# DVE normalises the three residual row tiles of a vision block, the context of tokens 3 and 4 is turned ahead of the later projections, and two orders change behind the router

## The chip, the core and the metric

The kernel runs on one core of a Trainium2 chip. The metric is the device time of one execution in microseconds. The core has TensorE (PE, matrix products and transposes, into eight PSUM banks), VectorE (DVE), ScalarE (ACT), GpSimd (POOL) and SyncE (SP, here the queue that issues most DMAs). Each engine runs its own instructions strictly in program order and waits on semaphores for the others. So what an engine does next is decided by the order in which its code is written.

## The reference

A patch tokeniser with local and global attention makes five tokens for each of 64 images; a class token is put ahead. Then a block of attention and a mixture of experts follows, and this is where the change lies:

```python
h = _L0_tok_ref(...)                                  # tokens by convolution and two small attentions
h = jnp.concatenate([cls, h], axis=1)                 # 6 tokens of 256 for each of 64 images
h = h + _L0_attn_ref(_layernorm(h, axis=-1), Wq, Wk, Wv, Wp, bp)
h = h + _L0_ffn_ref(_layernorm(h, axis=-1), gate_w, gate_up_w, down_w)

# in _L0_attn_ref
ctx = jnp.einsum('bhqk,bhkd->bqhd', w, v).reshape(b, t, D_OUT)
return ctx @ Wp + bp
# in _L0_ffn_ref: 8 experts, each token goes to the 2 best
router_logits = x_flat @ gate_w
router_probs = jax.nn.softmax(router_logits, axis=-1)
top_k_probs, top_k_idx = jax.lax.top_k(router_probs, TOP_K)
gate_up = jnp.einsum('nd,edh->enh', x_flat, gate_up_w)
hidden = jax.nn.silu(gate_out) * up_out
expert_out = jnp.einsum('enf,efd->end', hidden, down_w)
```

`_layernorm` is (x - mean) / sqrt(variance + eps) over the 256 channels.

## The kernel before

**Tiles.** The 6 tokens of 64 images are 384 rows of 256 channels, kept as three row tiles of 128 rows: tile 0 holds tokens 1 and 2, tile 1 tokens 3 and 4, tile 2 tokens 0 and 5. After attention each row tile has its residual sum in a PSUM bank (6, 7 and 5).

**From attention to the router.** Attention runs in three blocks (`BLOCKS`): block 0 queries tokens 0 to 2, block 1 tokens 3 and 4, block 2 token 5. For each, DVE and POOL multiply probabilities with values (`token_values`, one line for both engines, L485), TensorE sums and turns the products into a context (`turn_context(k, bank)`, L881), ScalarE copies it out (`context_copy`, L1348), and TensorE projects it into the bank of a row tile (`out_proj(j)`, L890). `ctx1` is the context of tokens 3 and 4; only row tile 1 needs it.

**The residual's normalisation** (names `mid0`, `mid1`, `mid2`): DVE takes the moments of a row tile from its bank (`residual_moments`: L1678, L1682, L1685, the last writes `veps`, variance plus eps). POOL raises it to the power of -1/2 (`reciprocal_root`, L1515). For `mid2` DVE normalises from its bank with mean and root (L1692). For `mid0` and `mid1` POOL also makes the negative mean times the root (`negative_mean`, L1521) and ScalarE normalises (L1219). `midn` are the normalised rows, in the tile that the profile calls pe_rows.

**What needs the normalised rows.** TensorE turns them (`turn_mid`, L604); ScalarE casts the turned columns to the high part (`experts_input_hi`, L1354), copies the residual out of the bank (`residual_copy`, L1232) and casts the rows themselves (`token_rows_hi`, L1268); DVE subtracts for the low part of the columns (`experts_input_lo`, L1957); POOL copies the rows a second time (`second_rows`, L1599) and subtracts for the low part of the rows (`token_rows_lo`, L1579). The router (`router(j)`, L904) needs high and low columns of tile j. DVE also splits the weights of the first slot tile in this time (`tile_weights_lo`, L1963). Between them TensorE issues matmuls whose result nobody reads (`keep_clock(bank, n)`, L911).

**Behind the router.** The dense expert runs over all rows in four quarters: TensorE `gate_up(n)` (L982), ScalarE silu (L1425), DVE `hidden(n)` (L2075). `gate_up(n)` waits for `hidden(n-2)`. In the same time DVE ranks the logits and places each token in a slot (lines 2045 to 2125), POOL scatters the rows to DRAM, and the other experts run over 11 slot tiles of 128 rows. Slot tiles 0 and 1 are gathered on chip, the later ones are loaded back by SP behind the scatter, and the weights of slot tile 3 are issued behind those loads. For each slot tile s, TensorE does `tile_gate_up(s)` (L1053), `rows_turn(s + 1)` (L1038), `tile_out(s - 1)` (L1071), `give_back(s - 2)` (L1084) and `hidden_turn(s)` (L1062). `rows_turn` is followed by ScalarE's high part (L1432) and DVE's low part (L2136) of the rows, which the next `tile_gate_up` needs; `hidden_turn(s)` needs DVE's product of silu and up (L2145), which needs ScalarE's silu (L1439). ScalarE casts the weights of the next slot tile in the same queue (L1362).

Each engine's code is written out by hand, and that order is what the change edits. Each wait names a count of a semaphore; `wait_normed` waits for `act_normed` or `normed_done`, by the engine that normalises (`ACT_NORMED`, `NORMED`).

Of the kernel before, what the change touches and what calls it, by code (L numbers as in the profile page):

```python
# [26 lines left out]
C = 256  # L27
# [26 lines left out]
SHIFTED_LOGITS, MASKED, NUMBERED, PLACED, WEIGHED, ROUTED = 2, 6, 13, 19, 30, 33  # L54
VSTEPS = 5
REST = KCH[-1][1]
REST_PARTS = ((0, 64), (64, REST))
# [19 lines left out]
GATHERED = 2  # L77
# [10 lines left out]
def columns(items):  # L88
    at, out = 0, {}
    for name, width in items:  # L90
# [19 lines left out]
       "pool0", "in0", "pool1", "in1", "in2", "mid0", "mid2", "mid1"]  # L110
NORMED = ["red0", "class", "red1", "in2", "mid2"]
ACT_NORMED = ["in0", "in1", "mid0", "mid1"]
SHIFTED = ACT_NORMED

# [26 lines left out]
def tower_kernel(nc, xa, xb, conv_w, tok_w, att_w, consts, biases, rows, ffn_w, out):  # L141
    ctx = ExitStack()
    with ctx:
# [274 lines left out]
        def wait_rstd(eng, name):  # L418
            eng.wait_ge(rstd_done, LNS.index(name) + 1)
# [82 lines left out]
        def _(sp):  # L502
# [25 lines left out]
            def tile_a(s):  # L528
                if s == 1:
                    sp.wait_ge(pool_values, BLOCKS[0][1] + 2)  # L530
                    sp.wait_ge(dve_values, 2)
                if s == 2:
                    sp.wait_ge(a_split, FQ)
                if s >= RING:
                    sp.wait_ge(tile_a_split, FQ * (s - RING + 1))
                sp.dma_start(a_ring[ring(s)].rearrange("p q n -> p (q n)"), expert_of(s)[:, 0:FQ * FFN_A]).then_inc(tile_a_in[s % RING], 16)
# [34 lines left out]
        def _(pe):  # L571
# [381 lines left out]
            pe.wait_ge(pool_values, BLOCKS[0][1] + 1)  # L953
            turn_context(2, 1)
            out_proj(2, [(3, "ctx0"), (1, "ctx2")])
            pe.wait_ge(pool_values, BLOCKS[0][1] + 2)
            pe.wait_ge(dve_values, 2)
            turn_mid(0, 3)
            turn_context(1, 4)
            turn_mid(2, 1)  # L960
            out_proj(1, [(4, "ctx1")])
            pe.wait_ge(gate_split, 1)
# [146 lines left out]
            for s in range(SLOT_TILES):  # L1109
                tile_gate_up(s)  # L1110
                if s == 0:
                    down(0, 7)
                if s == 1:
                    pe.wait_ge(rows_split, GATHERED)
                    down(1, 2)
                if GATHERED < s + 1 < SLOT_TILES:
                    rows_turn(s + 1)
                if s:
                    tile_out(s - 1)
                if s > 1:  # L1120
                    give_back(s - 2)
                if s + 1 == GATHERED:
                    rows_turn(s + 1)
                hidden_turn(s)
# [7 lines left out]
        def _(act):  # L1132
# [88 lines left out]
            def in_normalise(j):  # L1221
                normalise(inn[:, j, :], bank[ROW_BANK[j]][:, 0:C], f"in{j}").then_inc(act_normed, 1)

            def mid_normalise(j):
                normalise(midn[:, j, :], bank[ROW_BANK[j]][:, 0:C], f"mid{j}").then_inc(act_normed, 1)

# [177 lines left out]
            context_copy(2, 1)  # L1404
            mid_normalise(0)
            experts_input_hi(0, 3)
            residual_copy(0)
            token_rows_hi(0)
            context_copy(1, 4)
            experts_input_hi(2, 1)  # L1410
            residual_copy(2)
            token_rows_hi(2)
            mid_normalise(1)
            experts_input_hi(1, 4)
# [72 lines left out]
        def _(pool):  # L1487
# [158 lines left out]
            reciprocal_root("mid0", 1)  # L1646
            negative_mean("mid0")
            pool.tensor_copy(xrow[:, :, :, ROW_TOKEN], spread(token_of[:, :], 2, PICKS)).then_inc(rows_ready, 1)
# [7 lines left out]
            reciprocal_root("mid1", 1)  # L1656
            negative_mean("mid1")
            second_rows(1)
# [14 lines left out]
        def _(dve):  # L1673
# [92 lines left out]
            def row_moments(j):  # L1766
                dve.wait_ge(h_full, j + 1)
                moments(f"in{j}", [bank[ROW_BANK[j]][:, 0:C]])

            def residual_moments(j):  # L1770
                b = ROW_BANK[j]
                wait_full(dve, b, f"wp{j}")
                moments(f"mid{j}", [bank[b][:, 0:C]])
# [256 lines left out]
            residual_moments(0)  # L2030
            wait_rstd(dve, "mid0")
            tile_weights_lo(0, 0)
            tile_weights_lo(0, 1)
            residual_moments(2)
            experts_input_lo(0, 3)
            normalise("mid2", [bank[ROW_BANK[2]][:, 0:C]], [midn[:, 2, :]])
            experts_input_lo(2, 1)
            residual_moments(1)
            wait_rstd(dve, "mid1")
            tile_weights_lo(0, 2)  # L2040
# [49 lines left out]
            dve.tensor_tensor(ahead[:, :, :, :], spread(over[:, :, :], 1, SPARSE), spread(before, 3, MOST), ALU.mult).then_inc(route_step, 1)  # L2090
            dve.tensor_tensor(slot[:, :, :], counts[:, 0:RT, :], spread(near_first[:, :], 1, RT), ALU.add).then_inc(route_step, 1)
            dve.wait_ge(route_step, 15)
            dve.tensor_reduce(first_tile[:, :], ahead[:, :, :, :].rearrange("p e f t -> p e (f t)"), AX.X, ALU.add).then_inc(route_step, 1)
# [7 lines left out]
            dve.tensor_tensor(slot1[:, :, :], slot[:, :, :], fmask, ALU.mult).then_inc(route_step, 1)  # L2101
            hidden(1)
            for j in range(RT):
# [154 lines left out]
```

## Time and profile before

| | before |
|---|---|
| median of 3 runs | 213.39 us (213.3 to 215.37) |
| profiled execution, its own time | 213.47 us |
| span of the profiled execution, first to last instruction | 211.7 us |
| mean granted TensorE clock | 0.995 of full speed |
| busy, share of the span: TensorE / its weight loads | 92% / 80% |
| busy: DVE / ScalarE / POOL | 66% / 51% / 38% |
| DMA | 32.90 MB, mean 155 GB/s |

The profile records one execution. A group row gives line, engine, operation, output and input; then busy time and the mean of one. A timeline row gives start, duration and, in brackets, the idle time ahead of it and what ended that. The chain of waits follows the last instruction back to whatever released it at each step. Matmuls in fp32 are recorded as two passes each, so two instructions of 256 columns show as x4. Matmul ends include the pipeline's tail, so rows overlap a little.

### The profile page before, as it was taken

The numbers are of one execution on the slowest core, as the hardware profiler recorded it, in microseconds if no ns is written. First come the engines' busy times: TensorE is split into PE (matmuls) and PEld (weight loads), VectorE is DVE, ScalarE is ACT, GpSimd is POOL, SyncE is SP. The second block draws the span as 40 slices with busy tenths as digits, with TensorE's granted clock in tenths as the row PEclk, the third lists the DMA queues.
The fourth block names the chain that finished last, engine by engine and source line by source line (L and its number), as shares of the span: only waits on it lengthen the run. The fifth ranks groups of instructions, "written<-read, shape, count | busy, mean of one in ns | idle before, by whom it ended". The sixth has DMA issues, their size and how long they took to land.

```text
span 211.7 us, 3444 instructions
## 1 busy us (share of the span) xinstructions
PE 194.5 (92%) x1142; PEld 169.7 (80%) x1142; DVE 140.1 (66%) x338; ACT 108.7 (51%) x235; POOL 80.6 (38%) x108
## 2 busy tenths in 40 slices
PE   1999999999999998898967999999999999999991
PEld 1899999998897885876956878988788888888871
DVE  1664976385999998755897448646588677666411
ACT  3575294555327355434831434244487676777320
POOL 4027165274474030366059644485032211122220
PEclk9999999999999999999999999999999999999997
DMA  6999997000491000000004800124999988843003
GB/s 214 339 383 400 303 317 213 3 0 0 138 413 49 0 3 0 0 0 2 3 0 136 362 0 2 37 91 131 374 384 369 326 302 315 301 134 101 0 0 74
DMA packets 10189, 32.90 MB, mean 155 GB/s; under 512 B 1190, under 2 KB 5628, under 8 KB 8508
## 3 DMA queue, kind: packets, MB, share of 16 engines
q1 hardware_dynamic: 8120, 29.53, 39.5%
q10 hardware_dynamic: 1764, 2.37, 3.4%
q0 software_dynamic: 288, 0.79, 1.0%
q8 instruction: 9, 0.15, 0.3%
q14 instruction: 8, 0.07, 0.1%
HBM read 30.05 MB, written 2.64 MB: 154 GB/s over the span
## 4 chain that ended last, share of the span: by engine, by line
PE 66%; DVE 17%; issue 4%; ACT 3%; DMA 3%; POOL 3%; SPq 2%; ACTq 0%; DVEq 0%
PE bank L1053 14%; PE bank L580 10%; PE bank L1071 9%; PE bank L657 6%; PE bank L1084 4%; PE bank L982 3%; DMA raw<-xb 3%; PE bank L992 2%; PE bank L1062 2%; PE bank L604 2%; DVE stats L1678 2%; DVE split L1802 2%; DVE kv_rows L1732 1%; PE bank L722 1%; SPq L468 1%
## 5 line engine op out<-in xcount | busy, mean ns | idle before, releaser
L1053 PE MATMUL bank<-split 128*128 128x512 f32 x132 | 33.2, 400 | 0.5 <-DVE split L2136 0.5
L1611 POOL TENSOR_SCALAR split<-token_row,window 128x384 fp32r<-128x384 f32 x11 | 15.4, 1398 | 46.3 <-PE bank L1084 46.3
L580 PE MATMUL bank<-split 128*128 128x256 f32 (+1 forms) x225 | 28.3, 285 | 0.2 <-DVE split L1804 0.2
L1053 PEld LDWEIGHTS bank<-split 128*128 128x128 f32 x132 | 24.0, 188 | 5.5 <-DVE split L2136 0.7
L580 PEld LDWEIGHTS bank<-split 128*128 128x128 f32 (+1 forms) x225 | 27.5, 191 | 0.5 <-DVE split L1804 0.3
L657 PE MATMUL bank<-split 128*128 128x512 f32 x108 | 26.5, 397 | 0.0
L1515 POOL TENSOR_TENSOR rstd<-veps,mhalf 128x1 f32<-128x1 f32 (+2 forms) x17 | 14.2, 835 | 27.9 <-DVE veps L1685 27.6
L657 PEld LDWEIGHTS bank<-split 128*128 128x128 f32 x108 | 19.8, 188 | 3.9
L1963 DVE TENSOR_TENSOR split<-raw,split 128x512 fp32r<-128x512 f32 x28 | 18.4, 697 | 6.6 <-ACT split L1362 5.2
L1535 POOL TENSOR_TENSOR window<-window,pe_rows 128x256 f32<-128x256 f32 x14 | 14.5, 1034 | 8.6 <-ACT pe_rows L1140 8.0
L1362 ACT CAST split<-raw 128x512 fp32r<-128x512 f32 x28 | 16.5, 620 | 1.9 <-DMA raw<-ffn_w 1.9
L1202 ACT ACTIVATE kv_rows<-bank,rstd 128x512 f32<-128x512 f32 x18 | 12.1, 689 | 10.1 <-PE bank L657 9.3
L1140 ACT COPY pe_rows<-bank 128x256 f32<-128x256 f32 x18 | 6.5, 373 | 18.7 <-PE bank L580 17.6
L2145 DVE TENSOR_TENSOR kv_rows<-bank,kv_rows 128x512 f32<-128x512 f32 x11 | 7.6, 690 | 11.8 <-PE bank L1053 9.1
L595 PE MATMUL bank<-split 128*128 128x256 f32 (+1 forms) x45 | 8.6, 369 | 5.1 <-ACT split L1154 5.1
L1963 DVE TENSOR_TENSOR split<-kv_rows,split 128x512 fp32r<-128x512 f32 x16 | 11.1, 735 | 2.0 <-ACT split L1362 1.9
L595 PEld LDWEIGHTS bank<-split 128*128 128x128 f32 (+1 forms) x45 | 8.1, 275 | 5.4 <-ACT split L1154 5.4
L1084 PE MATMUL bank<-split 128*128 128x256 f32 x66 | 11.5, 309 | 0.7 <-DVE split L2151 0.7
L1802 DVE TENSOR_TENSOR split<-raw,split 128x1536 fp32r<-128x1536 f32 x5 | 8.8, 1754 | 4.9 <-ACT split L1163 4.9
L1678 DVE BATCH_NORM_STATS2 stats<-pe_rows 128x6 f32<-128x256 f32 x18 | 6.5, 414 | 8.1 <-ACT pe_rows L1140 8.1
L1084 PEld LDWEIGHTS bank<-split 128*128 128x128 f32 x66 | 9.2, 189 | 1.7 <-DVE split L2151 1.2
L1362 ACT CAST split<-kv_rows 128x512 fp32r<-128x512 f32 x16 | 9.5, 620 | 0.5 <-DMA kv_rows<-ffn_w 0.5
(274 smaller groups left out, 400.4 us busy)
## 6 DMA issues: line engine op xcount, KB each, us to landing
raw<-ffn_w SPq DMA_DIRECT2D x7, 1024.0 KB, 7.5
kv_rows<-ffn_w SPq DMA_DIRECT2D x4, 1024.0 KB, 7.2
raw<-xa SPq DMA_DIRECT2D x5, 768.0 KB
raw<-ffn_w SPq DMA_DIRECT2D x7, 512.0 KB, 8.5
kv_rows<-ffn_w SPq DMA_DIRECT2D x4, 512.0 KB, 6.8
tok<-tok_w SPq DMA_DIRECT2D x1, 1536.0 KB, 12.6
raw<-ffn_w SPq DMA_DIRECT2D x1, 1536.0 KB, 6.4
expert_rows<-zero_row SPq DMA_DIRECT2D x1, 1419.0 KB, 12.9
```

Source lines behind the costliest of these rows:

```text
L580: mm = pe.matmul(bank[b][:, 0:C], xs[0:n, g % 2, px, a:a + P], cws[0:n, pw, k, :], start=(k == 0 and m == 0), stop=(k == len(KCH) - 1 and ...
L595: mm = pe.matmul(bank[j][:, 0:C], xs[0:n, 0, px, a:a + P], cws[0:n, pw, k, :], start=(k == 0 and m == 0), stop=(k == len(KCH) - 1 and m == 2))
L657: mm = pe.matmul(bank[b][:, :], lns[:, g % 2, px, a:a + P], wkvs[:, pw, aw:aw + 2 * C], start=(c == 0 and m == 0), stop=(c == CC - 1 and m ...
L1053: mm = pe.matmul(bank[half][:, :], xst[:, s % 2, px, c * P:(c + 1) * P], tile_aws[s % 2][:, piece, pw, :], start=(c == 0 and m == 0), stop ...
L1071: mm = pe.matmul(bank[6][:, 0:C], hcols[s % 2][:, q * P:(q + 1) * P], b_ring[ring(s)][:, q, :], start=(q == 0), stop=(q == FQ - 1))
L1084: mm = pe.matmul(bank[SUM_BANK[j]][:, 0:C], back[:, s % 2, j * P:(j + 1) * P], eo[:, s % 2, px, :], start=(s == 0 and px == HI), stop=(s = ...
L1362: act.copy(tile_aws[s % 2][:, piece, HI, :].rearrange("p (q n) -> p q n", q=FQ), a_ring[ring(s)][:, :, piece * P:(piece + 1) * P]).then_in ...
L1515: pool.tensor_tensor(rstd[0:parts, k, 0:n], veps[0:parts, k, 0:n], mhalf[0:parts, 0:n], ALU.pow).then_inc(rstd_done, 1)
L1535: pool.tensor_tensor(redsum[:, wt, :], pe_rows[:, wt, 0, :] if n == 1 else redsum[:, wt, :], pe_rows[:, wt, n, :], ALU.add).then_inc(sum_s ...
L1611: pool.tensor_scalar(back[:, s % 2, :], token_row[:, :], xr[:, s % ROW_RING, ROW_TOKEN:ROW_TOKEN + 1], None, ALU.is_equal).then_inc(back_d ...
L1802: dve.tensor_tensor(xs[:, g % 2, LO, 0:n], x_raw[:, g % RAW_X, 0:4, :].rearrange("p k n -> p (k n)"), xs[:, g % 2, HI, 0:n].bitcast(F32), ...
L1963: dve.tensor_tensor(tile_aws[s % 2][:, piece, LO, :].rearrange("p (q n) -> p q n", q=FQ), a_ring[ring(s)][:, :, piece * P:(piece + 1) * P] ...
```

## The change

The three normalisations all go to DVE, which loses its waits for the roots at those places in exchange for the operation itself; POOL makes no negative mean for them and ScalarE does not normalise. TensorE's order ahead of the router is changed, ScalarE copies `ctx1` directly behind the other two, and DVE takes the moments of tile 1 ahead of the normalisations of tiles 2 and 1. Behind the router `hidden(1)` is placed earlier in DVE's routing steps, and `rows_turn(2)` is placed ahead of `tile_out(0)`. `DVE_VALUES = 2` names a number that was written out.

```diff
-NORMED = ["red0", "class", "red1", "in2", "mid2"]
-ACT_NORMED = ["in0", "in1", "mid0", "mid1"]
+NORMED = ["red0", "class", "red1", "in2", "mid0", "mid2", "mid1"]
+ACT_NORMED = ["in0", "in1"]
@@ TensorE
             turn_context(2, 1)
+            pe.wait_ge(pool_values, BLOCKS[0][1] + 2)
+            pe.wait_ge(dve_values, DVE_VALUES)
+            turn_context(1, 4)
             out_proj(2, [(3, "ctx0"), (1, "ctx2")])
-            pe.wait_ge(pool_values, BLOCKS[0][1] + 2)
-            pe.wait_ge(dve_values, 2)
+            out_proj(1, [(4, "ctx1")])
             turn_mid(0, 3)
-            turn_context(1, 4)
             turn_mid(2, 1)
-            out_proj(1, [(4, "ctx1")])
             pe.wait_ge(gate_split, 1)
@@ TensorE, slot tiles
-                if GATHERED < s + 1 < SLOT_TILES:
+                if GATHERED <= s + 1 < SLOT_TILES:
                     rows_turn(s + 1)
                 if s:
                     tile_out(s - 1)
                 if s > 1:
                     give_back(s - 2)
-                if s + 1 == GATHERED:
-                    rows_turn(s + 1)
                 hidden_turn(s)
@@ ScalarE
             context_copy(2, 1)
-            mid_normalise(0)
+            context_copy(1, 4)
             experts_input_hi(0, 3)
             residual_copy(0)
             token_rows_hi(0)
-            context_copy(1, 4)
             experts_input_hi(2, 1)
             residual_copy(2)
             token_rows_hi(2)
-            mid_normalise(1)
             experts_input_hi(1, 4)
@@ POOL
             reciprocal_root("mid0", 1)
-            negative_mean("mid0")
...
             reciprocal_root("mid1", 1)
-            negative_mean("mid1")
             second_rows(1)
@@ DVE
+            def mid_normalise(j):
+                normalise(f"mid{j}", [bank[ROW_BANK[j]][:, 0:C]], [midn[:, j, :]])
...
             residual_moments(0)
-            wait_rstd(dve, "mid0")
+            mid_normalise(0)
             tile_weights_lo(0, 0)
             tile_weights_lo(0, 1)
             residual_moments(2)
+            residual_moments(1)
+            mid_normalise(2)
+            mid_normalise(1)
             experts_input_lo(0, 3)
-            normalise("mid2", [bank[ROW_BANK[2]][:, 0:C]], [midn[:, 2, :]])
             experts_input_lo(2, 1)
-            residual_moments(1)
-            wait_rstd(dve, "mid1")
             tile_weights_lo(0, 2)
             tile_weights_lo(0, 3)
             experts_input_lo(1, 4)
@@ DVE, routing
             dve.tensor_tensor(slot[:, :, :], counts[:, 0:RT, :], spread(near_first[:, :], 1, RT), ALU.add).then_inc(route_step, 1)
+            hidden(1)
             dve.wait_ge(route_step, 15)
...
             dve.tensor_tensor(slot1[:, :, :], slot[:, :, :], fmask, ALU.mult).then_inc(route_step, 1)
-            hidden(1)
             for j in range(RT):
```

TensorE between attention and router. L881 is the context (x6 for block 2, x9 for tokens 3 and 4), L890 the projection, L604 the turn of a normalised tile, L904 the router, L911 the clock keepers. Before:

```order
L881 MATMUL bank<-con,window 128x128 x6
L890 MATMUL bank<-att,pe_rows 128x256 x2
L604 MATMUL bank<-con,pe_rows 128x128 x2
L881 MATMUL bank<-con,window 128x128 x9
L604 MATMUL bank<-con,pe_rows 128x128 x2
L890 MATMUL bank<-att,pe_rows 128x256 x2
L904 MATMUL bank<-gsplit,split 128x8 x12
L911 MATMUL bank<-att,con 128x256 x4
L604 MATMUL bank<-con,pe_rows 128x128 x2
L911 MATMUL bank<-att,con 128x256 x2
L904 MATMUL bank<-gsplit,split 128x8 x6
```

And of the change, where the same lines are numbered one higher:

```order
L882 MATMUL bank<-con,window 128x128 x15
L891 MATMUL bank<-att,pe_rows 128x256 x4
L605 MATMUL bank<-con,pe_rows 128x128 x4
L905 MATMUL bank<-gsplit,split 128x8 x12
L912 MATMUL bank<-att,con 128x256 x4
L605 MATMUL bank<-con,pe_rows 128x128 x2
L912 MATMUL bank<-att,con 128x256 x2
L905 MATMUL bank<-gsplit,split 128x8 x6
```

Both contexts, both projections and both turns now stand together; router, keepers and the last turn stand as before.

DVE at the same place, from the moments of tile 0 on. L1963 are weight splits, L1957 the low part of turned columns, L1692 the normalisation. Before:

```order
L1685 TENSOR_SCALAR veps<-mv 128x1
L1963 TENSOR_TENSOR split<-raw,split 128x512 x2
L1678 BN_STATS stats<-bank 128x6
L1682 BN_AGGR mv<-stats 128x2
L1685 TENSOR_SCALAR veps<-mv 128x1
L1957 TENSOR_TENSOR split<-bank,split 128x2x128
L1692 TENSOR_SCALAR pe_rows<-bank,mv,rstd 128x256
L1957 TENSOR_TENSOR split<-bank,split 128x2x128
L1678 BN_STATS stats<-bank 128x6
L1682 BN_AGGR mv<-stats 128x2
L1685 TENSOR_SCALAR veps<-mv 128x1
L1963 TENSOR_TENSOR split<-raw,split 128x512 x2
```

And of the change:

```order
L1677 TENSOR_SCALAR veps<-mv 128x1
L1684 TENSOR_SCALAR pe_rows<-bank,mv,rstd 128x256
L1958 TENSOR_TENSOR split<-raw,split 128x512 x2
L1670 BN_STATS stats<-bank 128x6
L1674 BN_AGGR mv<-stats 128x2
L1677 TENSOR_SCALAR veps<-mv 128x1
L1670 BN_STATS stats<-bank 128x6
L1674 BN_AGGR mv<-stats 128x2
L1677 TENSOR_SCALAR veps<-mv 128x1
L1684 TENSOR_SCALAR pe_rows<-bank,mv,rstd 128x256 x2
L1952 TENSOR_TENSOR split<-bank,split 128x2x128 x2
L1958 TENSOR_TENSOR split<-raw,split 128x512 x2
```

The low parts of tiles 0 and 2 stand behind the normalisation of tile 1, where they stood ahead of its moments.

POOL, of the change, from the root of mid0 (L1509) to that of mid1; L1567 is a weight split, L1593 `second_rows`, L1573 `token_rows_lo`:

```order
L1509 TENSOR_TENSOR rstd<-veps,mhalf 128x1
L1641 COPY pe_rows<-token_of 128x6
L1567 TENSOR_TENSOR split<-raw,split 128x512
L1509 TENSOR_TENSOR rstd<-veps,mhalf 128x1
L1644 MEMSET vprod 128x4x62
L1593 COPY pe_rows<-pe_rows 128x256
L1573 TENSOR_TENSOR split<-pe_rows,split 128x256
L1593 COPY pe_rows<-pe_rows 128x256
L1573 TENSOR_TENSOR split<-pe_rows,split 128x256
L1509 TENSOR_TENSOR rstd<-veps,mhalf 128x1
L1593 COPY pe_rows<-pe_rows 128x256
```

Here only the two negative means (one behind the first root, one behind the last) are gone; nothing else moved.

## Rows read from the trace of the kernel before

**Rows 1.** Chain of waits, 111 to 124 us: start, duration, engine, tile, line.
```profile
111.43 1.70 POOL window L485
113.84 1.29 POOL nmr L1521
115.15 0.57 ACT pe_rows L1219
121.59 1.29 POOL nmr L1521
```

**Rows 2.** Timeline of TensorE ahead of the router: start, duration, work, idle before.
```profile
112.07 1.50 PE L881 MATMUL bank<-con,window 128*128 128x128 f32 x12
...
116.22 2.17 PE L881 MATMUL bank<-con,window 128*128 128x128 f32 x18
118.23 0.38 PE L604 MATMUL bank<-con,pe_rows 128*128 128x128 f32 x2
...
119.63 1.58 PE L904 MATMUL bank<-gsplit,split 128*128 128x8 f32 x12
121.08 1.97 PE L911 MATMUL bank<-att,con 128*128 128x256 f32 x8
...
124.88 0.83 PE L904 MATMUL bank<-gsplit,split 128*128 128x8 f32 x6
```

**Rows 3.** Timeline of DVE ahead of the router.
```profile
115.16 0.43 DVE L1678 BATCH_NORM_STATS2 stats<-bank 128x6 f32<-128x256 f32 x1
...
115.85 0.15 DVE L1685 TENSOR_SCALAR veps<-mv 128x1 f32<-128x1 f32 x1
116.82 0.42 DVE L1957 TENSOR_TENSOR split<-bank,split 128x256 fp32r<-128x256 f32 x1 [0.82 <-ACT split L1354]
117.16 0.54 DVE L1692 TENSOR_SCALAR pe_rows<-bank,mv,rstd 128x256 f32<-128x256 f32 x1
...
121.53 1.29 DVE L1963 TENSOR_TENSOR split<-raw,split 128x512 fp32r<-128x512 f32 x2 [0.67 <-POOL rstd L1515]
```

**Rows 4.** Timeline of POOL ahead of the router.
```profile
117.54 0.73 POOL L1579 TENSOR_TENSOR split<-pe_rows,split 128x256 fp32r<-128x256 f32 x1
...
120.94 0.56 POOL L1515 TENSOR_TENSOR rstd<-veps,mhalf 128x1 f32<-128x1 f32 x1 [0.48 <-DVE veps L1685]
```

**Rows 5.** Timeline of ScalarE ahead of the router.
```profile
118.70 0.38 ACT L1354 CAST split<-bank 128x256 fp32r<-128x256 f32 x1
...
119.23 0.43 ACT L1268 CAST split<-pe_rows 128x256 fp32r<-128x256 f32 x1
```

**Rows 6.** Behind the router: timelines of TensorE, ScalarE, DVE; two pieces of the chain.
```profile
132.07 2.02 PE L982 MATMUL bank<-split 128*128 128x322 f32 x12 [0.35 <-DVE vprod L2075]
...
142.83 2.74 PE bank L1053 x12
...
150.17 3.03 PE L1053 MATMUL bank<-split 128*128 128x512 f32 x12 [0.48 <-DVE split L2136]
...
153.44 0.62 ACT L1362 CAST split<-raw 128x512 fp32r<-128x512 f32 x1 [1.90 <-DMA raw<-ffn_w]
...
154.70 0.68 DVE L2145 TENSOR_TENSOR kv_rows<-bank,kv_rows 128x512 f32<-128x512 f32 x1
...
155.85 0.44 PE bank L1062 x4
```

**Rows 7.** Page: clock, two groups; TensorE's last row; a window (its clock ahead of DMA).
```profile
PEclk9999999999999999999999999999999999999997
...
L580 PE MATMUL bank<-split 128*128 128x256 f32 (+1 forms) x225 | 28.3, 285 | 0.2 <-DVE split L1804 0.2
...
L595 PE MATMUL bank<-split 128*128 128x256 f32 (+1 forms) x45 | 8.6, 369 | 5.1 <-ACT split L1154 5.1
...
206.72 0.97 PE L1084 MATMUL bank<-split 128*128 128x256 f32 x6 [0.66 <-DVE split L2151]
...
209.50:210.00 0.50, 0.00 (x0) 0.00 (x0) 0.00 (x0) 0.00 (x0) 0.00 (x0) 0.50 0.91 219
```

More of the change, by code:

```diff
@@ L55 @@
 VSTEPS = 5
+DVE_VALUES = 2
 REST = KCH[-1][1]
@@ L530, in tile_a @@
                     sp.wait_ge(pool_values, BLOCKS[0][1] + 2)
-                    sp.wait_ge(dve_values, 2)
+                    sp.wait_ge(dve_values, DVE_VALUES)
                 if s == 2:
@@ L1222, in in_normalise @@
                 normalise(inn[:, j, :], bank[ROW_BANK[j]][:, 0:C], f"in{j}").then_inc(act_normed, 1)
-            def mid_normalise(j):
-                normalise(midn[:, j, :], bank[ROW_BANK[j]][:, 0:C], f"mid{j}").then_inc(act_normed, 1)
             def residual_copy(j):
```

## The prediction

> **What bounds the kernel now.** I began with the chain of waits, the view that follows the end back from step to step. Between attention and router (111 to 125.6 us) it does not run on TensorE: it goes through POOL's value product, POOL's inverse root and negative mean, and ScalarE's normalisation for row tile 0, then through the context of tokens 3 and 4, and a second time through the same POOL and ScalarE pair for row tile 1 [rows 1]. One negative mean of 128 numbers costs 1.29 us, twice. Then I read each engine's timeline there, because the change reorders four queues: TensorE [rows 2], DVE [rows 3], POOL [rows 4], ScalarE [rows 5]. In TensorE's rows see that the context of tokens 3 and 4 (L881 x18) starts at 116.22 only because the turn of mid0 stands ahead of it, though its values were done at 113.13; and that the last part of the router starts at 124.88. Behind the router I read the two places at which TensorE stands: 0.35 us for DVE's `hidden(1)`, 0.48 us for the rows of slot tile 2 [rows 6]. Last, the granted clock [rows 7].
>
> The sum is made against the profiled execution, 213.47 us (span 211.7), 0.08 above the median of 213.39.
>
> **The change, part by part.** A TensorE pass of 128 columns takes 0.112 us (18 from 116.22 to 118.23), one of 256 columns 0.22 (8 in 1.97 with their tail), the twelve small router passes 1.45 [rows 2]. A hand-over between engines takes 0.03 to 0.09 us.
>
> *Removed:* two negative means (2 x 1.29) and two ScalarE normalisations (2 x 0.57) [rows 1]. *Added:* two DVE normalisations at 0.54 [rows 3]. For mid0 alone this saves 1.3 us: its root is there when the negative mean starts, 113.84, so it is normalised by 114.4 and not 115.72. But that tile is no longer asked for then.
>
> *TensorE's new order.* The context of block 2 issues 12 passes from 112.07 to 113.41 [rows 2]; tokens 3 and 4 are ready by then, so their 18 passes run to 115.42 (results 115.58), not from 116.22: 2.8 us earlier. The projection of row tile 2 runs 115.42 to 116.29 (results 116.5); ScalarE's copy (0.38, as its cast of the same size [rows 5]) is done at 116.0, so the projection of row tile 1 follows, to 117.15 (results 117.38; before, it began at 118.9). Only then mid0 is turned: done at 117.53, where it was done at 116.38.
>
> *DVE.* The moments of a tile take 0.84 (115.16 to 115.85 and 0.15) [rows 3]: tile 2 from 116.54 to 117.38, tile 1 to 118.29. Both are now ahead of both normalisations. The root for mid2 is there at 118.0, so mid2 is normalised 118.27 to 118.81. Next in DVE's queue is the normalisation of mid1.
>
> *The new wait.* POOL's queue was not reordered: the root of mid1 stands behind `token_rows_lo(2)`, as the order shows. That waits for ScalarE's `token_rows_hi(2)`, which is the last of three ScalarE steps behind the turn of mid2. Step by step: turn of mid2 118.87 to 119.25; ScalarE's three steps (0.96 together, from the start at 118.70 to the end of the third, 119.23 and 0.43, in the kernel before) [rows 5] to 120.24; POOL's low part 0.73 from 120.31 to 121.04 and the root 0.56 to 121.56 [rows 4]; DVE normalises mid1 121.59 to 122.13. In the kernel before this root waited for the moments, not for the queue, and cost nothing extra. What is now queued behind the waiting instruction on DVE is `experts_input_lo` of tiles 0 and 2 (0.42 each) [rows 3], and the router waits for them: `experts_input_lo(0)` ends at 122.47, before 117.24. So TensorE stands from 119.25 to 122.53 with nothing between. Then, in its own queue, comes what used to lie under the wait for mid1: two routers 1.45 to 123.98, four clock keepers 8 x 0.22 to 125.71, the turn of mid1 (results 126.09), ScalarE 0.38 and DVE 0.42 in turn, 126.95, and the last router at 127.01. It was 124.88 [rows 2]. **Loss ahead of the router: 2.13 us.** DVE's two weight splits (1.29) [rows 3] lie under this.
>
> *Two orders behind the router.* `hidden(1)` moves ahead of five small steps, so the fourth `gate_up` needn't wait: TensorE gains 0.35. The steps that it passes are pushed back 0.4 us, but feed the scatter, which TensorE doesn't wait for until slot tile 2. `rows_turn(2)` moves ahead of `tile_out(0)`: ScalarE and DVE prepare the rows under 1.73 us of matmuls, and the third `tile_gate_up` starts 0.48 earlier and runs 2.74 as the second does, not 3.03: 0.77. Together 1.12 [rows 6]. But ScalarE then stands 1.90 us for the weights of slot tile 3 until 153.44, and TensorE's `hidden_turn(2)` needs the product that ends at 154.70 + 0.68 = 155.38 [rows 6]; it started at 155.85. That load is issued behind the scatter and does not come sooner relative to the router. So I keep 0.40 of the 1.12. **Gain: 0.40**, bounds 0 and 1.12.
>
> Sum without the clock: 213.47 + 2.13 - 0.40 = **215.2**.
>
> *The clock.* The page's clock row stays at 9 or more in tenths through all slices with matmuls. TensorE's last matmuls end at 207.69, after a pause of 0.66, and the granted clock is 0.50 from 209.5 to 210 [rows 7]. That is at most 1.8 us behind the end of work, and the new standstill lasts 3.3 us, behind 1.3 us more with nothing and one turn of 0.38. No row behind the first 5 us shows a standstill this long, so none shows the clock kept through one. The fall goes from the level of 2.4 GHz to that of 1.2, and work there takes up to twice its time. From below the cost is 0 (no fall). From above: the kernel's first 45 matmuls, out of a standstill (L595), take 8.6 us, and 45 of the same shape later (L580) 28.3 / 5 = 5.7 [rows 7], 2.9 more, waits for input included. TensorE is the bound from 122.5 on, so nothing hides it. I take 2.1, between the ends, which is also the distance of the slowest run shown (215.37) from the fastest (213.3); that those differ by such a lapse is not shown.
>
> The Trainium skill (TensorE: Matmul & The Clock Gate, HAM oscillation) says that a gap in TensorE's work drops it to half clock, and that the work behind the gap starts there. The trace agrees at the tail, 0.50 after the end of work, and shows no case in mid-kernel. By that rule the sum is 217.3, by the full clock that the mid-kernel slices show 215.2.
>
> **Forecast and rivals.**
> 1. *Standstill and clock fall*: 215.2 + 2.1 = 217.3, own range 216.0 to 219.0. Chance 0.60.
> 2. *Standstill, clock kept*: 215.2, from 214.4 (all of the 1.12 kept) to 215.9. For it: the full clock in every slice of the body. Chance 0.28.
> 3. *The changed order does what it says*, the other side: POOL gets to the root of mid1 as soon as the moments are there. Then the root ends at 118.9, mid1 is normalised at 119.5, the router starts at 120.0, keepers end at 123.2, the last router starts at about 124.5: 0.4 gained, and 0.4 behind the router, 212.7. It decides where the root ends by about 119.7 (rather than 121.56). Against it: the order of POOL's queue. Chance 0.06.
> 4. *Losses and gains cancel*: the standstill is covered in part (the split on POOL or ScalarE's three steps shorter than before) and the full 1.12 is kept: within 1 us of before, 214.0. Chance 0.06.
>
> The likeliest is 217.3. The range 214.5 to 219.0 leaves out rival 3, most of 4 and the top of the first. About 1% (2.1 us, so 215.5) is what a measurement of this kernel can tell from no change. Slower by more: 0.58 of the first and 0.10 of the second, 0.68; faster by more 0.04; the rest 0.28.
>
> **What would show it.** Right: DVE idle from about 118.8 for POOL's root, some 2.8 us; POOL's third root starting near 121.0, just behind its second low part; TensorE idle about 3.3 us ahead of the first router passes; the last router at 127; the third `tile_gate_up` without the wait for DVE; ScalarE's wait for tile 3's weights longer than 1.90; a granted clock under 1 somewhere in 119 to 129, router and keeper passes at twice their time. Wrong: no DVE wait for the root; a clock of 1.00 throughout (then rival 2); or `hidden_turn(2)` not waiting for the product, which would mean the weights came earlier.

## The result, and the profile after

The changed kernel takes 217.64 us (median, 217.47 to 218.82) against 214.0 for the kernel before beside it (213.3 to 215.37): the ratio is 1.0174, 95% interval 1.0106 to 1.0242. Forecast were 217.3 us in a range of 214.5 to 219.0. The profiled execution takes 217.56 us, 4.09 more than the one before, and its span is 4.0 longer.

The page of the changed kernel, its span, busy times and clock row:

```profile
span 215.7 us, 3440 instructions
...
PE 196.8 (91%) x1142; PEld 172.2 (80%) x1142; DVE 141.0 (65%) x340; ACT 107.8 (50%) x233; POOL 76.2 (35%) x106
...
PEclk9999999999999999999999769999999999999998
```

POOL and ScalarE do less, as meant; DVE has 340 instructions where it had 338. But the clock row has a 7 and a 6 in slices 23 and 24 (from 118.6 to 129.4 us), where the row of before has nines up to its last slice [rows 7].

The chain of waits of the changed kernel between attention and the dense expert (start, duration, engine, tile, line). Lines are one higher on TensorE and 4 to 8 lower elsewhere: L882 is the context, L605 the turns, L905 the router (L912, below, the keepers), L1684 DVE's normalisation, L1509 POOL's root, L1573 POOL's low part:

```profile
112.33 3.35 PE bank L882 x30
...
118.28 0.46 DVE pe_rows L1684
...
118.79 0.45 PE bank L605 x2
...
120.29 0.72 POOL split L1573
121.02 0.52 POOL rstd L1509
...
121.56 0.55 DVE pe_rows L1684
...
122.59 2.69 PE bank L905 x12
...
129.80 0.83 PE bank L905 x6
```

The negative means and ScalarE's normalisations of [rows 1] are gone. In their place the chain goes from TensorE's turn of mid2 (118.79) over three ScalarE steps and POOL's low part to POOL's root of mid1 (121.02), although that root needs nothing of this: it needs the moments, done at 118.28. What brings it there is the order of POOL's queue. The timeline of the changed kernel, POOL's rows first, then DVE's, then TensorE's, shows the three sides of it:

```profile
120.29 0.72 POOL L1573 TENSOR_TENSOR split<-pe_rows,split 128x256 fp32r<-128x256 f32 x1 [0.54 <-ACT split L1264]
120.97 0.56 POOL L1509 TENSOR_TENSOR rstd<-veps,mhalf 128x1 f32<-128x1 f32 x1
...
121.56 0.55 DVE L1684 TENSOR_SCALAR pe_rows<-bank,mv,rstd 128x256 f32<-128x256 f32 x1 [2.83 <-POOL rstd L1509]
122.03 0.75 DVE L1952 TENSOR_TENSOR split<-bank,split 128x256 fp32r<-128x256 f32 x2
...
122.59 2.69 PE L905 MATMUL bank<-gsplit,split 128*128 128x8 f32 x12 [3.36 <-DVE split L1952]
125.14 3.52 PE L912 MATMUL bank<-att,con 128*128 128x256 f32 x8
...
129.80 0.83 PE L905 MATMUL bank<-gsplit,split 128*128 128x8 f32 x6
```

DVE waits 2.83 us for the root, with the low parts of the router's input behind the waiting instruction, and TensorE waits 3.36 us for those. Then the same twelve router passes take 2.69 us where they took 1.58, and the eight keeper passes 3.52 where they took 1.97 [rows 2]. The stretches of 2 us, TensorE's busy time first and the granted clock third from the end, say why:

```profile
120.00:122.00 2.00, 0.00 (x0) 0.00 (x0) 0.43 (x1) 0.21 (x1) 1.24 (x2) 0.86 0.55 234
122.00:124.00 2.00, 1.41 (x7) 1.45 (x7) 1.97 (x5) 0.00 (x0) 0.40 (x1) 0.50 0.00 0
...
128.00:130.00 2.00, 1.95 (x11) 1.33 (x9) 0.42 (x1) 0.95 (x3) 0.05 (x1) 0.93 0.00 0
```

The granted clock is at its lower level, 1.2 GHz, from about 121.5 to 128.3 (the two stretches left out stand at 0.50 too), and at the upper one, 2.4 GHz, behind it. The Trainium skill (TensorE: Matmul & The Clock Gate, HAM oscillation) lets a gap in TensorE's work bring the clock down and has the work behind the gap start slow; this trace agrees, in mid-kernel too.

### The profile page after: what moved, and what is told of

Its sections match the earlier page's. It is cut to its first block, busy times and chain, and to the rows that moved or that the text cites. A ratio compares the mean times of both kernels' runs of the same rounds, so it can differ in the third digit from the quotient of the medians.

```text
span 215.7 us, 3440 instructions
## 1 busy us (share of the span) xinstructions
PE 196.8 (91%) x1142; PEld 172.2 (80%) x1142; DVE 141.0 (65%) x340; ACT 107.8 (50%) x233; POOL 76.2 (35%) x106
## 4 chain that ended last, share of the span: by engine, by line
PE 62%; DVE 16%; DMA 7%; issue 5%; POOL 4%; ACT 3%; SPq 1%; DVEq 0%; ACTq 0%; POOLq 0%
PE bank L1054 10%; PE bank L581 10%; PE bank L1072 7%; PE bank L658 6%; PE bank L1085 3%; PE bank L596 3%; DMA raw<-ffn_w 3%; DMA raw<-xa 2%; POOL expert_rows L1597 2%; PE bank L882 2%; DVE stats L1670 2%; PE bank L1063 2%; PE bank L605 2%; PE bank L983 2%; PE bank L905 2%
## 5 line engine op out<-in xcount | busy, mean ns | idle before, releaser
L1605 POOL TENSOR_SCALAR split<-token_row,window 128x384 fp32r<-128x384 f32 x11 | 14.1, 1281 | 47.1 <-PE bank L1085 47.1
L1509 POOL TENSOR_TENSOR rstd<-veps,mhalf 128x1 f32<-128x1 f32 (+2 forms) x17 | 14.2, 833 | 29.9 <-DVE veps L1677 29.6
L1958 DVE TENSOR_TENSOR split<-raw,split 128x512 fp32r<-128x512 f32 x28 | 19.0, 717 | 6.7 <-ACT split L1358 6.7
```

Source lines behind the costliest of these rows:

```text
L1509: pool.tensor_tensor(rstd[0:parts, k, 0:n], veps[0:parts, k, 0:n], mhalf[0:parts, 0:n], ALU.pow).then_inc(rstd_done, 1)
L1605: pool.tensor_scalar(back[:, s % 2, :], token_row[:, :], xr[:, s % ROW_RING, ROW_TOKEN:ROW_TOKEN + 1], None, ALU.is_equal).then_inc(back_d ...
L1958: dve.tensor_tensor(tile_aws[s % 2][:, piece, LO, :].rearrange("p (q n) -> p q n", q=FQ), a_ring[ring(s)][:, :, piece * P:(piece + 1) * P] ...
```

## The experiments

Eleven more kernels ran. Times are medians; the ratio is to the kernel before on the same chip, with its 95% interval (it is worked out from the runs, and is not exactly the quotient of two medians). The kernel before had medians of 213.86 us on the chip of x1 to x4, 214.24 on that of x5, x8, x9 and x10, and 214.06 on that of x6, x7 and x11. A ratio whose interval ends just below 1 (x3, x5, x6, x7) is a small gain at best. "Last router" is the start of its last six passes in the profiled execution, "rest" the span from there to the end.

| kernel | us | ratio to before | last router | rest |
|---|---|---|---|---|
| before (first profile) | 213.39 | 1 | 124.88 | 86.8 |
| the change | 217.64 | 1.0174 (1.0106 to 1.0242) | 129.80 | 85.9 |
| x1_root_ahead | 213.76 | 0.9985 (0.9956 to 1.0014) | 127.16 | 86.6 |
| x2_filled | 215.55 | 1.0086 (1.0045 to 1.0128) | 128.42 | 85.5 |
| x8_norm_behind | 213.51 | 0.9947 (0.991 to 0.9984) | 126.04 | 85.6 |
| x10_root_filled | 211.41 | 0.9855 (0.9789 to 0.992) | 124.58 | 85.5 |
| x4_ahead_only | 218.93 | 1.0253 (1.016 to 1.0345) | 129.97 | 87.2 |
| x3_behind_only | 213.28 | 0.9954 (0.9921 to 0.9988) | 124.65 | 86.1 |
| x6_hidden_only | 213.44 | 0.9969 (0.9942 to 0.9996) | 126.83 | 86.2 |
| x7_turn_only | 213.44 | 0.9968 (0.9941 to 0.9994) | 125.06 | 86.0 |
| x5_dve_norm_only | 213.16 | 0.9951 (0.9912 to 0.999) | 123.95 | 86.9 |
| x9_best | 209.2 | 0.9749 (0.9683 to 0.9815) | 121.8 | 85.8 |
| x11_best_bare | 212.25 | 0.9929 (0.9899 to 0.9958) | 122.0 | 88.2 |

The start of this stretch moves by up to 2 us between profiled executions of kernels that are equal up to there (the context of block 2 begins at 112.07 in the first profile of before, at 114.02 in that of x6_hidden_only), so a router's start is compared within its own trace where it matters. The profiles of x2_filled and x6_hidden_only, the two that start latest, have a fall of the clock of their own far ahead, which before and the change have not (x6_hidden_only, the clock third from the end):

```profile
16.00:18.00 2.00, 2.00 (x11) 2.00 (x11) 0.51 (x5) 0.00 (x0) 0.90 (x1) 0.50 0.94 393
```

One profiled execution need not be the median one: that of x1_root_ahead took 215.66 us and was the slowest of its eleven. For the last two kernels all eighteen router passes run in one block, and the start of the last six is an estimate, that of the block and two thirds of its passes.

**The root ahead.** One line of POOL moves:

```diff
             reciprocal_root("mid2", 1)
+            reciprocal_root("mid1", 1)
             pool.memset(hidf[:, :, 0:FIRST], 0.0).then_inc(hid_zero, 1)
...
             token_rows_lo(2)
-            reciprocal_root("mid1", 1)
             second_rows(1)
```

> The change with one line of POOL moved: the root of mid1 straight behind the root of mid2, ahead of the row copies and low parts. Theory A (POOL's queue order makes the standstill): the root starts near 118.4 instead of 120.97, DVE's wait of 2.83 us for it shrinks below 0.8, TensorE's idle time ahead of the first router passes falls from 3.36 to about 0.8, the clock stays up, the last router starts near 124.5, time 212.5 (211.8 to 213.3), faster than before. Theory B (the loss comes from DVE's own extra work or from the contexts being ahead of the turns): the time stays within 0.6 of the changed kernel, 217 to 218.

Measured 213.76 us: 3.9 less than the change. POOL's root, DVE's wait and TensorE's wait of x1_root_ahead:

```profile
118.42 0.55 POOL L1509 TENSOR_TENSOR rstd<-veps,mhalf 128x1 f32<-128x1 f32 x1 [0.32 <-DVE veps L1677]
...
119.01 0.54 DVE L1684 TENSOR_SCALAR pe_rows<-bank,mv,rstd 128x256 f32<-128x256 f32 x1 [0.21 <-POOL rstd L1509]
...
118.85 0.44 PE L605 MATMUL bank<-con,pe_rows 128*128 128x128 f32 x2 [1.16 <-DVE pe_rows L1684]
120.03 1.94 PE L905 MATMUL bank<-gsplit,split 128*128 128x8 f32 x12 [0.74 <-DVE split L1952]
121.82 3.76 PE L912 MATMUL bank<-att,con 128*128 128x256 f32 x8
...
127.16 1.17 PE L905 MATMUL bank<-gsplit,split 128*128 128x8 f32 x6
```

Theory B falls: the queue's order made the standstill, and moving one instruction takes it away as foretold (waits 0.21 and 0.74). But my expectation also named a clock that stays up, a last router at 124.5 and at most 213.3 us, and all three were wrong. The keepers still take 3.76, and the clock is down (0.50 from 122 to 126) with no pause longer than 1.16 us ahead of the fall. That is no quirk of the one profiled execution, though the others lost less: their mean granted clock is 0.982 to 0.991, and the nine with 0.986 or more took 213.01 to 213.91. Two of the stretches of x1_root_ahead:

```profile
118.00:120.00 2.00, 0.44 (x2) 0.20 (x3) 1.75 (x6) 1.35 (x6) 1.69 (x5) 1.00 1.08 451
120.00:122.00 2.00, 1.97 (x13) 2.00 (x14) 1.61 (x3) 0.27 (x1) 2.00 (x3) 0.71 0.62 250
```

Between the turn of mid0, which ends at 117.68, and the fall near 120.9 TensorE did one turn (two passes of 128 columns, 0.44 us) and some of the twelve router passes of 8 columns, nothing more. So there are two losses, the wait and the fall of the clock, and the fall doesn't need the long standstill.

**The standstill filled.** The change, no wait taken away, seven keepers more:

```diff
             wait_free(pe, 2, "router")
+            keep_clock(0, 7)
             router(0, 3)
```

> The change with seven more clock keepers (matmuls whose result nobody reads, 14 passes of 0.22 us, 3.0 us) ahead of the first router, in the standstill. No wait is taken away. Theory A (standstill costs 2.1 us, and the clock's fall another 2.7 on top): granted clock 1.00 from 116 to 130, last router near 127.1 instead of 129.80, time 214.9 (214.3 to 215.6). Theory C (the fall costs nothing because padding matmuls absorb it): no change, 217.3 to 217.9.

Measured 215.55, 2.1 less than the change with 3 us more matmuls; my 214.9 was a little low, its range just held. The granted clock was 1.00 in every stretch of 2 us from 112 to 132, and the lengths are those of before again (timeline of x2_filled):

```profile
120.52 3.19 PE L912 MATMUL bank<-att,con 128*128 128x256 f32 x14
123.95 1.50 PE L905 MATMUL bank<-gsplit,split 128*128 128x8 f32 x12 [0.24 <-DVE split L1953]
125.31 1.97 PE L912 MATMUL bank<-att,con 128*128 128x256 f32 x8
```

Theory C falls. From the start of the two projections (L891) to the last router it is 128.42 - 116.97 = 11.45 us, in the change 129.80 - 115.51 = 14.29: the fall costs 2.8 us in these two executions.

**Both.** The root ahead and four keepers around the turn of mid2:

```diff
             turn_mid(0, 3)
+            keep_clock(0, 2)
             turn_mid(2, 1)
+            keep_clock(0, 2)
```

> The change with POOL's root of mid1 straight behind that of mid2, and with four more clock keepers: two between the turns of mid0 and mid2, two behind the turn of mid2, where TensorE has nothing else for 1.16 and 0.74 us. The kernel with the root alone still lost its clock. Theory A (what is left there is the clock alone): granted clock 1.00 from 116 to 130, last router near 124.8 instead of 127.16, time 211.7 (211.0 to 212.4) against 213.8 without keepers. Theory D (the clock falls for another reason than idle matmul time here, so keepers only add): 213.8 to 214.5.

Measured 211.41, inside the range, 2.4 below x1_root_ahead though it does 1.7 us of matmuls more. The granted clock is 1.00 in every stretch of 2 us from 112 to 132; the router passes of x10_root_filled:

```profile
120.14 1.47 PE L905 MATMUL bank<-gsplit,split 128*128 128x8 f32 x12
...
124.58 0.83 PE L905 MATMUL bank<-gsplit,split 128*128 128x8 f32 x6
```

From the projections to the last router: 8.90, x1_root_ahead 11.59. With both losses gone the change is 1.5% faster than the kernel before.

**The normalisation behind.** POOL as in the change, and DVE's order mended instead:

```diff
             mid_normalise(2)
-            mid_normalise(1)
             experts_input_lo(0, 3)
             experts_input_lo(2, 1)
+            mid_normalise(1)
```

> The change with POOL's order left as it is and DVE's normalisation of mid1 moved behind the low parts of tiles 0 and 2. If the loss is what stands behind the waiting instruction on DVE, this heals the standstill as well as the POOL edit does, though the root is still late (about 121): first router passes near 119.9 instead of 122.59, TensorE's wait there below 0.9 us; the clock falls as with the POOL edit (same idle time ahead), last router near 127, time 213.8 (213.2 to 214.6). If the late root itself is the loss, the time stays at 217 or more.

Measured 213.51. The root is as late (5.5 us behind the start of the projections, as in the change), but the router does not wait for it (timeline of x8_norm_behind, DVE and TensorE):

```profile
122.37 0.54 DVE L1684 TENSOR_SCALAR pe_rows<-bank,mv,rstd 128x256 f32<-128x256 f32 x1 [1.47 <-POOL rstd L1509]
...
120.02 1.77 PE L905 MATMUL bank<-gsplit,split 128*128 128x8 f32 x12
```

So the harm was what stood behind the wait on DVE, not the late root. Either queue mends it. The clock fell here as well (0.61 from 122 to 124, 0.53 from 124 to 126), later and for less. Nine of its ten executions have a mean granted clock of 0.983 to 0.992 and took 212.96 to 213.94 us; the tenth, at 0.996, took 211.27. It is as fast as x10_root_filled. So the price of the fall shows here too, about 2 us, with no edit in between.

**Ahead only, behind only, and its two parts.** The change without its two orders behind the router; the kernel before with these alone; and each of them alone. The two edits, as x6_hidden_only (DVE) and x7_turn_only (TensorE) make them in the kernel before; x3_behind_only makes both, x4_ahead_only takes both out of the changed kernel:

```diff
             dve.tensor_tensor(slot[:, :, :], counts[:, 0:RT, :], spread(near_first[:, :], 1, RT), ALU.add).then_inc(route_step, 1)
+            hidden(1)
...
             dve.tensor_tensor(slot1[:, :, :], slot[:, :, :], fmask, ALU.mult).then_inc(route_step, 1)
-            hidden(1)
```

```diff
-                if GATHERED < s + 1 < SLOT_TILES:
+                if GATHERED <= s + 1 < SLOT_TILES:
                     rows_turn(s + 1)
...
-                if s + 1 == GATHERED:
-                    rows_turn(s + 1)
                 hidden_turn(s)
```

> The change without the two orders behind the router; all edits ahead of it stand. Theory A: the whole loss is here, last router at about 129.8 with the same standstill of 3.4 us and the same clock fall, time 218.5 (217.9 to 219.2), that is above the changed kernel by what the two orders bring (0.4 to 1.1). If the two orders cost time, it is below 217.6.

> The kernel before with only the two orders behind the router (hidden(1) ahead of five routing steps, rows_turn(2) ahead of tile_out(0)). My sum kept 0.40 of 1.12 us because the weights of slot tile 3 bound it: 213.0. If the weights come sooner by themselves, as the trace of the changed kernel hints (6.24 us to land instead of 7.08), 0.8 to 1.1 us: 212.4. If the orders bring nothing: 213.4.

> The kernel before with hidden(1) ahead of five routing steps, nothing else. TensorE's wait of 0.35 us for it goes (row L982 [0.35 <-DVE vprod]). If the later waits for rows and weights don't give it back: 0.3 to 0.4 faster; if rows_turn(2), which waits for DVE and for rows behind the scatter, takes it back: 0 to 0.1.

> The kernel before with rows_turn(2) ahead of tile_out(0), nothing else. Ceiling 0.77 us (no wait for DVE ahead of the third tile_gate_up, which then runs 2.74 instead of 3.03). Both orders together gave 0.74 us in the traces and 0.58 between medians. If this order carries nearly all: 0.5 to 0.8 faster.

Measured: 218.93; 213.28 (median 0.6 below before); 213.44 and 213.44 (0.6 each, where I expected 0.3 to 0.4 of the first). The whole loss lies ahead of the router, and the two orders are worth about 1 us: the rest of the span is 87.2 without them and 85.9 with them in the changed kernel, 86.8 and 86.1 in the kernel before. `hidden(1)` alone gives 86.2, `rows_turn(2)` alone 86.0; their sum would be more than both together give in x3_behind_only. Its trace shows why. With both waits gone TensorE comes to `rows_turn(2)` before the rows that SP loads back behind the scatter:

```profile
146.90 0.44 PE L1038 MATMUL bank<-con,window 128*128 128x128 f32 x2 [0.40 <-DMA window<-expert_rows]
```

In x2_filled, x8_norm_behind and x10_root_filled, which have both orders and no such wait, the rest is 85.5 to 85.6, that is 1.2 to 1.3 less than before. In x6_hidden_only the fourth gate_up follows the third without a wait (L982 x24 in one row), in x7_turn_only the third tile_gate_up has lost its wait. The timelines of TensorE, x6_hidden_only first, then x7_turn_only:

```profile
131.64 3.83 PE L982 MATMUL bank<-split 128*128 128x322 f32 x24
...
151.55 3.01 PE L1053 MATMUL bank<-split 128*128 128x512 f32 x12 [0.49 <-DVE split L2136]
```

```profile
149.63 3.00 PE L1053 MATMUL bank<-split 128*128 128x512 f32 x12
```

**DVE normalises, nothing else.** In the kernel before, DVE takes over both normalisations where it stood and waited for the root; POOL's negative means and ScalarE's two `mid_normalise` go:

```diff
-NORMED = ["red0", "class", "red1", "in2", "mid2"]
-ACT_NORMED = ["in0", "in1", "mid0", "mid1"]
+NORMED = ["red0", "class", "red1", "in2", "mid0", "mid2", "mid1"]
+ACT_NORMED = ["in0", "in1"]
...
-            wait_rstd(dve, "mid0")
+            normalise("mid0", [bank[ROW_BANK[0]][:, 0:C]], [midn[:, 0, :]])
...
-            wait_rstd(dve, "mid1")
+            normalise("mid1", [bank[ROW_BANK[1]][:, 0:C]], [midn[:, 1, :]])
```

> The kernel before with one part of the change alone: DVE normalises mid0 and mid1 at the two places where it waited for their roots; all queues keep their order, POOL's negative means and ScalarE's two normalisations are gone. Both legs get shorter by about 1.1 and 0.8 us; last router near 123.1 instead of 124.88, the rest unchanged: 212.0 (211.4 to 212.8), faster than before by 0.9%. If the DVE normalisation is the harmful part: above 213.9.

Measured 213.16, ratio 0.9951: 0.5% less (interval 0.1 to 0.9) where I expected 0.9, and outside my range. Its timeline shows where the rest went, DVE and POOL first:

```profile
114.41 2.02 DVE L1959 TENSOR_TENSOR split<-raw,split 128x512 fp32r<-128x512 f32 x2
114.01 1.27 POOL L1571 TENSOR_TENSOR split<-raw,split 128x512 fp32r<-128x512 f32 x1
...
116.35 0.42 DVE L1674 BATCH_NORM_STATS2 stats<-bank 128x6 f32<-128x256 f32 x1
...
118.44 0.44 PE L604 MATMUL bank<-con,pe_rows 128*128 128x128 f32 x2 [0.92 <-DVE pe_rows L1688]
```

Without the negative mean POOL's weight split begins 1.2 us earlier (before, at 115.22) and now lies beside DVE's two, which take 2.02 instead of 1.29 [rows 3]. The moments of tile 2 begin at 116.35 instead of 115.16 [rows 3]: 0.7 of this is the longer splits, most of the rest DVE's new normalisation ahead of them. The turn of mid2 waits 0.92 us for DVE. That POOL's split slows DVE's is read from this lengthening; no run kept them apart with all else the same. POOL's own is not slowed: it takes 1.27 here and 1.26 apart, in the kernel before. The idea of the change, a shorter way through the normalisation, is not what loses time.

**A version that beats both.** The root ahead; the turn of mid1 directly behind that of mid2; the six keepers that stood between the routers become four around the turns; on DVE the low part of tile 1 between the two weight splits:

```diff
             turn_mid(0, 3)
+            keep_clock(0, 2)
             turn_mid(2, 1)
+            keep_clock(0, 1)
+            turn_mid(1, 4)
+            keep_clock(0, 1)
...
             router(2, 1)
-            keep_clock(0, 4)
-            turn_mid(1, 4)
-            keep_clock(0, 2)
...
             tile_weights_lo(0, 2)
-            tile_weights_lo(0, 3)
             experts_input_lo(1, 4)
+            tile_weights_lo(0, 3)
```

> Towards a version that beats both: the change with POOL's root of mid1 early, the turn of mid1 directly behind the turn of mid2, and the six keepers that stood between the routers spread as two, one and one around the turns; on DVE the low part of tile 1 between the two weight splits. Theory A: the last router starts near 121.7 instead of 129.80 (124.88 before), the clock stays up, about 0.8 us behind the router are kept: 209.7 (209.0 to 211.0). If the clock falls here too (the routers are narrow matmuls), 211.5 to 213.

> The fastest version so far (209.2 us) without its four keepers. If the keepers hold the clock there: the granted clock falls near 121, gate_up runs at half pace for several us, time 211.5 (210.8 to 213). If the clock holds without them: 209.0 to 209.4, since one of them stands in the way for about 0.2.

Measured 209.2 us, ratio 0.9749; and 212.25 without the four keepers, 3 us more for leaving 1.7 us of work out. The two kernels differ in nothing else. How the 2.2 us between x10_root_filled and x9_best divide among the other edits (the turn of mid1, six keepers fewer between the routers, DVE's order) was not measured. TensorE's timeline of x9_best, then of x11_best_bare, where the granted clock is 0.52 from 122 to 124 and 0.50 from 124 to 128:

```profile
117.75 1.03 PE L912 MATMUL bank<-att,con 128*128 128x256 f32 x4
119.08 0.44 PE L605 MATMUL bank<-con,pe_rows 128*128 128x128 f32 x2 [0.30 <-DVE pe_rows L1685]
119.36 0.60 PE L912 MATMUL bank<-att,con 128*128 128x256 f32 x2
119.84 0.44 PE L605 MATMUL bank<-con,pe_rows 128*128 128x128 f32 x2
120.12 0.60 PE L912 MATMUL bank<-att,con 128*128 128x256 f32 x2
120.36 2.25 PE L905 MATMUL bank<-gsplit,split 128*128 128x8 f32 x18
122.48 3.84 PE L984 MATMUL bank<-split 128*128 128x322 f32 x24
```

```profile
120.47 2.50 PE L905 MATMUL bank<-gsplit,split 128*128 128x8 f32 x18
122.83 6.53 PE L981 MATMUL bank<-split 128*128 128x322 f32 x24
```

The first two gate_ups take 3.84 us with the keepers and 6.53 without: the same matmuls at the two clock levels.

## Why the prediction was right, step by step

- **TensorE's new order.** Two contexts in one row of 30 passes from 112.16, projections 115.51, turn of mid0 117.24: each within 0.1 us of the working. All of this trace stands 0.09 later than the first.
- **The new wait.** Root foretold 121.0 to 121.56, found 120.97 and 0.56; DVE's idle 2.8, found 2.83; TensorE's 3.3, found 3.36; first router 122.53, found 122.59. x1_root_ahead and x8_norm_behind show it by undoing it from either side.
- **The clock.** Foretold as likely, at 2.1 us between 0 and 2.9. It fell, and costs 2.7 by the last router (129.80, where 127.01 and the 0.09 would be 127.1), 2.8 by x2_filled. The 2.1 was mis-sized: I took it from the spread of three runs, which shows nothing of it. The upper bound of 2.9 from the kernel's first matmuls lies near the measured value, but the profile shows a granted clock of 1.00 for them (all of 4 to 20 us), so no row shows that they ran at the lower level, and the nearness proves nothing. My ground for the fall, a standstill longer than any seen, was too narrow: x1_root_ahead fell without one.
- **Behind the router.** Foretold a gain of 0.40 out of 1.12, found 0.9 (86.8 to 85.9). The step that failed is the cap by the weights of slot tile 3, which took 0.72 of the 1.12 away and measured 0.2 to 0.3. The mechanism is there: `hidden_turn(2)` starts at 159.59, right behind the product that waits for these weights, 0.3 us later than the matmuls ahead of it would let it. But the load takes 6.24 us here where I carried over 7.08 (chain of waits of the changed kernel):

```profile
151.33 6.24 DMA raw<-ffn_w
157.59 0.63 ACT split L1358
...
159.59 0.66 PE bank L1063 x4
```

In the traces of the experiments the same load, from issue to ScalarE's cast, takes 5.0 (x3_behind_only, 146.45 to 151.45) to 6.5 us (x4_ahead_only). The single value of before, issued at 146.36 and used at 153.44 [rows 6], was the longest of all. I treated one draw as a constant. Where the load took 5.0 to 5.1 us (x2_filled, x8_norm_behind, x10_root_filled) the whole 1.12 was there, and in x3_behind_only, at 5.0 too, the wait of 0.40 for the rows was the limit, to which my sum had given no price.
- **DVE's weight splits.** I carried 1.29 us for two over from [rows 3]. The first pair, beside POOL's split as in x5_dve_norm_only, takes 2.02 here, 0.7 more. It hides under the wait for the projection of tile 2 (the moments wait 0.23 for TensorE at 116.58), so the sum didn't feel it.
- **The sum.** 2.1 + 2.7 - 0.9 = 3.9 of the 4.0 us. The forecast of 3.8 had two errors against one another, 0.6 too little for the clock and 0.5 too little gained. So the path was foretold, step by step, and that the sum of 217.3 came within 0.4 us of 217.64 is luck.
- **Rivals.** Rival 2 (clock kept) is what x2_filled forced, 1.0086. Rival 3 (the order does what it says) got its condition, an early root, in x1_root_ahead: the clock fell there, for which this rival had no term, and it took 213.8 where I wrote 212.7. With the clock held, in x10_root_filled, the last router starts at 124.58, foretold 124.5, and the time is 211.4. Rival 4 needed a standstill covered in part, and it was 3.36 us, not covered.

## What to carry to other kernels

When a wait moves ahead of other work on an in-order engine, look up where its releaser stands in *its* queue, not when its input is ready: here the root's input was ready at 118.28 and the root came at 120.97, because the queue that makes it was not reordered with the queue that uses it. Look again at where padding matmuls stand when the order around them changes: four around the turns, where TensorE had nothing but turns between waits, were worth 3 us (x9_best against x11_best_bare), while the change kept six between the routers and lost its clock ahead of them. And a duration that comes from one transfer in one trace is a draw, not a bound.

## What the runs showed of the hardware

- TensorE's clock fell to 1.2 GHz with no pause above 1.16 us (x1_root_ahead), where for 2.3 us it had only one turn (0.44 us) and then router passes of 8 columns. Its longest pause in x10_root_filled is 0.30 in the same stretch, with passes of 256 columns, and the clock stays. Whether the pauses or the kind of passes made the difference is open: no run changed one of them alone.
- Once down the clock stayed there for 6.8 us in the change (121.5 to 128.3), through more than 5 us of router passes and keepers without a pause. In x11_best_bare it stayed down from 122 to 128 and beyond, under unbroken passes of 322 columns, and in x8_norm_behind for about 3.4 us (an estimate from 0.61 and 0.53 in two stretches of 2 us). At the low level 24 passes of 322 columns take 6.53 us instead of 3.84, twelve of 8 columns 2.69 instead of 1.47.
- One DVE split of 128x512 takes 0.68 us in the median, and 1.42 where POOL's split of the same form (113.93 to 115.20) lies beside it. All splits of this form in the changed kernel (duration in ns: least, median, most):

```profile
L1958 DVE TENSOR_TENSOR split<-raw,split x28: 674/684/1424, 114.3 to 194.7; 128x512 fp32r<-128x512 f32 x28
```

  The Trainium skill (GPSIMD Engine Reference, Specifications) names contention on the SBUF interface that POOL shares with DVE, for DVE instructions with two inputs there. This trace agrees, and puts the price at 0.7 us for this one, for DVE alone: POOL's split takes 1.27 beside it and 1.26 apart. In the kernel before the most was 0.99. The DMA traffic is not the reason: with the DMA engines at 0.75 in this stretch, three splits from 159.86 to 161.95 take 2.09 together at 1.00.
- The kernel before seems to have falls of the clock by itself: of its 73 runs beside the experiments, the ten with a mean granted clock of 0.986 or less have a median of 215.1 us, the others 213.9. None of these was traced. Where such a fall can lie shows in x6_hidden_only, equal to before up to there: 0.50 from 16 to 18 us, behind a pause of TensorE of 1.90 us, and 45 passes (L580) take 7.15 us from 15.09 on where they take 5.66 in before.
